# One array for rows and expert outputs, weights beside the last scatters, and the last batch in two halves

## What is computed

```python
x = x + tanh(g_xattn[0]) * attention(layernorm(x), ctx, ctx, bias=(b1 + b2 - b3) * side)   # 64 keys per batch
h = layernorm(x)
p = sigmoid(h @ Wr.T + rb)                       # 8 experts, the 2 best of each row, weighted by p
x = x + tanh(g_ffn[0]) * (expert(h, shared) + sum(p[e] * expert(h, e) for e in top2(p)))
        # expert(h, e) = (silu(h @ Wg.T) * (h @ Wu.T)) @ Wd.T, inner width 512
f = layernorm(x)
t = tanh(ctx @ Ws  [per text]  +  f @ W  [per row]  +  b)      # every row with each of 64 texts, 256 wide
att = softmax(t @ w + mask)
ws, bs = tanh(att @ ctx @ Wcw.T + bcw), tanh(att @ ctx @ Wcb.T + bcb)
x = x + tanh(g_xattn[1]) * (ws * f + bs)
q = clip(round(layernorm(x) / s), -127, 127)
x = x + tanh(g_ffn[1]) * (s * q @ (ternary - 1).T + bias)
```

## Time and profile before

| | |
|---|---|
| median of 3 runs | 1060.84 us (1059.93 to 1063.52) |
| profiled execution | 1066.61 us |
| its span | 1065.0 us |
| mean granted TensorE clock | 0.95 of full speed |
| busy share: TensorE, VectorE, ScalarE, GpSimd | 89%, 71%, 62%, 22% |
| one row tile's activation on ScalarE (L724) | 0.60 us |
| bytes moved by DMA | 220.81 MB |

### The profile page before, as it was taken

One profiled execution on the slowest core, in us unless ns is written; L12 is line 12 of the kernel. 1 busy time (PEld: TensorE's weight loads), 2 busy tenths in 40 slices (PEclk: granted clock), 3 DMA queues, 4 the chain that ended last, 5 costly groups with the idle time before them and its releaser, 6 DMA issues.

```text
span 1065.0 us, 22912 instructions
## 1 busy us (share of the span) xinstructions
PE 952.0 (89%) x8350; PEld 750.5 (70%) x8350; DVE 752.8 (71%) x2048; ACT 656.9 (62%) x893; POOL 229.8 (22%) x260
## 2 busy tenths in 40 slices
PE   5689998886999889999999999999999999986762
PEld 2447777675999877877777878878887887843331
DVE  2697777673222368879879969867875776697995
ACT  1122112110110029979999999969987986899991
POOL 1014344444012212122212312111211111120000
PEclk9689899998999999999999999999999999998886
DMA  8012999923999866656666666677776766410000
GB/s 262 25 55 97 396 407 390 340 70 135 333 349 327 295 224 232 231 171 223 207 220 218 216 219 229 235 244 239 272 259 217 256 229 228 150 32 21 2 21 21
DMA packets 138754, 220.81 MB, mean 207 GB/s; under 512 B 14129, under 2 KB 80178, under 8 KB 138642
## 3 DMA queue, kind: packets, MB, share of 16 engines
q1 hardware_dynamic: 120242, 157.59, 44.2%
q10 hardware_dynamic: 8464, 34.60, 8.3%
q0 software_dynamic: 9936, 27.15, 7.2%
HBM read 159.14 MB, written 60.16 MB: 206 GB/s over the span
## 4 chain that ended last, share of the span: by engine, by line
PE 50%; issue 6%; DVE 5%; DMA 1%; POOL 0%; POOLq 0%; DVEq 0%
PE bank L1289 20%; PE bank L1484 15%; PE bank L1458 10%; PE bank L1466 2%; PE bank L1411 1%; DVE tanhs L1132 1%; PE bank L1510 1%; PE bank L1336 1%; DVE arena L1132 0%; DMA picked<-expert_rows,slot_of 0%; DVE tanhs L1131 0%; DVE arena L1131 0%; DVE shared_w L1131 0%; DVE shared_w L1132 0%; DVE normed L912 0%
## 5 line engine op out<-in xcount | busy, mean ns | idle before, releaser
L1289 PE MATMUL bank<-rowsT,expert_w 128*128 128x128 f32 x2656 | 327.3, 277 | 1.9 <-issue 1.9
L1289 PEld LDWEIGHTS bank<-rowsT,expert_w 128*128 128x128 f32 x2656 | 318.0, 193 | 10.9 <-issue 7.4
L744 ACT ACTIVATE tanhs<-shared_w,txtT 128x512 f32<-128x512 f32 x268 | 169.7, 726 | 30.3 <-issue 19.8
L1458 PE MATMUL bank<-expert_w,act 128*128 128x256 f32 x664 | 160.7, 385 | 0.0
L645 POOL DMA_DIRECT2D expert_rows<-rows_out x71 | 44.7, 629 | 449.6 <-DVE rows_out L1089 425.5
L1458 PEld LDWEIGHTS bank<-expert_w,act 128*128 128x128 f32 x664 | 120.1, 190 | 30.3 <-issue 17.3
L744 ACT ACTIVATE arena<-shared_w,txtT 128x512 f32<-128x512 f32 x216 | 136.4, 728 | 0.0
L724 ACT ACTIVATE act<-bank 128x512 f32<-128x512 f32 x83 | 49.7, 599 | 131.5 <-PE bank L1289 126.6
L656 POOL DMA_INDIRECT picked<-expert_rows,slot_of x64 | 73.4, 1146 | 94.3 <-issue 55.4
L1089 DVE COPY rows_out<-bank 128x256 f32<-128x256 f32 x71 | 30.0, 422 | 89.5 <-PE bank L1458 89.4
L1484 PE MATMUL bank<-arena,pick_w 128*32 128x256 f32 x1320 | 85.8, 387 | 5.9 <-ACT arena L733 4.8
(11 more groups left out here) (267 smaller groups left out, 1414.3 us busy)
## 6 DMA issues: line engine op xcount, KB each, us to landing
expert_w<-in_WgT SPq DMA_DIRECT2D x71, 512.0 KB
expert_w<-in_WuT SPq DMA_DIRECT2D x71, 512.0 KB
expert_w<-in_WdT SPq DMA_DIRECT2D x71, 512.0 KB
expert_rows<-tanhs ACTq DMA_DIRECT2D x1, 33792.0 KB
rows_in<-rows_by_expert SPq DMA_DIRECT2D x71, 128.0 KB, 5.8
expert_rows<-rows_out POOLq DMA_DIRECT2D x71, 128.0 KB, 5.4
expert_w<-in_WgsT SPq DMA_DIRECT2D x12, 512.0 KB
expert_w<-in_WusT SPq DMA_DIRECT2D x12, 512.0 KB
```

Source lines behind the costliest of these rows:

```text
L744: got = e.activation(tiles[ec][:, S * j:S * (j + 1)], featT[ec], ACT.Tanh, bias=txtT[:, ec, t + j:t + j + 1])
L1289: got = e.matmul(bank[:, i * P:(i + 1) * P], w[:, at:at + P], t[:, c * P:(c + 1) * P], start=c == 0, stop=c == DC - 1)
L1458: got = e.matmul(row_bank[:, 0:D], act[n % 2][:, c * P:(c + 1) * P], w[:, at:at + D], start=c == 0, stop=c == IC - 1)
```

## The change

- The array `outs_dram` is gone. Expert outputs are stored to `rows_dram`, over the rows of their own tile, and gathered from there.
- `rows_dram` is set to zero before the scatters. `blank` now issues nine transfers on ScalarE's queue: for each batch b the part of all eight regions into which that batch's rows can be the first to come (4 MB), and the part for absent tiles (1 MB). They are placed at the start, ahead of the first attention steps. The scatters of batch b wait for part b, and the first fetch for the part of the absent tiles. `zero_rows`, `pads` and `pad` are gone, with their constants.
- The first `fetch` waits for the tile list and the constants, issues the weights of tiles 0 and 1, and only then waits for all scatters and loads rows.
- The last batch's second part is done in two groups of 256 rows. `groups` has nine entries in place of eight batches; the last two have 16 tanh tiles each, of 4 texts by 256 rows. `mix_in`, `feature`, `rho` and `mix_out` of such a group work on half the rows. The first half can begin when the first two of the batch's four row blocks are gathered, and its `mix_out` runs beside the second half's tanh tiles.
- `PAIRS`, `JOINS`, `PLACES` and `LAGS` have other values.

The diff, cut to its core:

```diff
-PAIRS = {0: 21, 1: 11, 2: 12, 3: 8, 4: 4, 5: 8, 6: 17, 7: 28}
-JOINS = {0: 8, 1: 8, 2: 8, 3: 16, 4: 19, 5: 12, 6: 1, 7: 0}
+PAIRS = {0: 17, 1: 12, 2: 10, 3: 0, 4: 0, 5: 0, 6: 18, 7: 24, 8: 10}
+JOINS = {0: 16, 1: 8, 2: 8, 3: 28, 4: 28, 5: 28, 6: 1, 7: 0, 8: 0}
...
+        self.groups = [(b, 0, ST) for b in range(B - 1)] + [(B - 1, 0, ST // 2), (B - 1, ST // 2, ST // 2)]
+        self.tiles = [T * n // 8 for _, _, n in self.groups]
...
+        tiles = self.tiles[g]
+        share = min(int(PAIRS[g]), tiles)
+        return m * share // tiles != (m + 1) * share // tiles
...
-        place([[("blank",)]], PLACES["blank"], PLACES["blank"])
+        place([[("blank",)]], -PLACES["att_norm"] - 19, -PLACES["att_norm"] - 19)
...
                     if r == 0:
                         e.wait_ge(s_tiles, 1)
-                        e.wait_ge(s_zeroed, 16)
-                        e.wait_ge(s_padded, 16 * E)
-                        for j in range(2):
-                            e.wait_ge(s_scattered[j], 32 * ST * B // 2)
+                        e.wait_ge(s_absent, 16)
...
-                    if r >= WEIGHTS:
+                        for q in range(2):
+                            fetch_weights(n_of[q])
+                        for j in range(2):
+                            e.wait_ge(s_scattered[j], 32 * ST * B // 2)
+                    elif r >= WEIGHTS:
...
                 elif name == "scatter":
                     b, i = k
                     e.wait_ge(s_placed, b + 1)
+                    if i == 0:
+                        e.wait_ge(s_zeroed[b], 16)
...
-                elif name == "pad":
-                    h, = k
-                    e.wait_ge(s_pads, 1)
-                    e.wait_ge(s_zero, 1)
-                    for j in range(h * E // 2, (h + 1) * E // 2):
-                        e.indirect_dma_start(
-                            out=rows_dram, out_offset=bass.IndirectOffsetOnAxis(ap=pad_at[:, j:j + 1], axis=0),
-                            in_=zero_tile[:, :], in_offset=None).then_inc(s_padded, 16)
...
-                    e.dma_start(outs_dram[bass.ds(tile * P, P), :], rows_out[r % OUTS][:, :]).then_inc(s_stored[r % OUTS], 16)
+                    e.dma_start(rows_dram[bass.ds(tile * P, P), :], rows_out[r % OUTS][:, :]).then_inc(s_stored[r % OUTS], 16)
...
                 elif name == "blank":
                     e.wait_ge(s_zeros, 1)
-                    e.dma_start(outs_dram.rearrange("(p n k) d -> p n (k d)", p=P, n=BLANKS),
-                                zeros.unsqueeze(1).to_broadcast([P, BLANKS, 1024])).then_inc(s_blank, 16)
+
+                    by_batch = rows_dram[0:ABSENT * P, :].rearrange("(e b p k) d -> b p e (k d)", e=E, b=B, p=P)
+                    for b in range(B):
+                        e.dma_start(by_batch[b], zeros.unsqueeze(1).to_broadcast([P, E, 1024])).then_inc(s_zeroed[b], 16)
+                    e.dma_start(rows_dram[ABSENT * P:, :].rearrange("(p n k) d -> p n (k d)", p=P, n=2),
+                                zeros.unsqueeze(1).to_broadcast([P, 2, 1024])).then_inc(s_absent, 16)
...
+                        cols_of, W = rows_of(g), P * groups[g][2]
+                        t = groups[g][0] * T + 2 * S // W * m
                         for ec in range(DC):
-                            for j in range(2):
-                                got = e.activation(tiles[ec][:, S * j:S * (j + 1)], featT[ec], ACT.Tanh, bias=txtT[:, ec, t + j:t + j + 1])
+                            for j in range(2 * S // W):
+                                got = e.activation(tiles[ec][:, W * j:W * (j + 1)], featT[ec][:, cols_of], ACT.Tanh,
+                                                   bias=txtT[:, ec, t + j:t + j + 1])
...
+                    for j in range(2 * S // W):
+                        got = e.tensor_scalar(w[:, W * j:W * (j + 1)], featT[ec][:, cols_of], txtT[:, ec, t + j:t + j + 1], None, ALU.add)
+                    got.then_inc(s_wide_in, 1)
```

More of the change, by code:

```diff
@@ L124, in route @@
             steps[-self.ST] += [("opened", 1)]
-            steps += [[("pads",)], [("tiles",)]] + [[("pad", h)] for h in range(2)]
+            steps += [[("tiles",)]]
         return steps
@@ L168, in added, with mix_out @@
[L168 to L176 removed]
+    def mix_out(self, g):
+        halves = range(self.groups[g][2] // 2)
+        return [[("rho", g)], [], [("turn_rho", g)], [("soft_rho", g)], [("rsum", g)], [("weigh_c", g)], [("squash", g)], [("stretch", g)],
+                [("power", "lin", g)], [("affine", g)], [("newton", "lin", g)], [("step", g)], *([("quantize", g, h)] for h in halves),
+                [("apply", g)], [("turn_q", g)], [("add_bias", g)], *([("linear", g, h)] for h in halves)]
```

503 lines of the change are left out of this document (269 added, 234 removed).

## The result

The changed kernel takes 1129.04 us (median; 1126.99 to 1131.62) against 1062.18 (1059.93 to 1066.47) for the kernel before on the same chip: a ratio of 1.0626, 95% interval 1.0583 to 1.0669. It is 66.9 us slower; the forecast was 18.7 us faster, and the range ended at 1061.

What follows compares the result with a forecast made beforehand. Bounds: TensorE and ScalarE in the batch stages, plus the 245 to 267 us seam. Terms -9.5 + 2 - 11.4 + 0.2 = -18.7 gave 1047.9 profiled, 1042 as median; range 1027 to 1061.

Steps and rivals of the forecast that it cites:

- 5.7 us in front of that copy: Start, ScalarE: nine zeroing issues at 0.63 us delay batch 0's first attention copy; taken as +4 us, bounds 0 and +6.
- a rival with 0.12: Start: ScalarE's queue holds it between zeroing issues, some 25 to 75 us later, 1068 to 1118, middle 1085; chance 0.12.
- Zeroing: First part: early zeroing issues cost +4 us, scatters no longer sharing the DMA engines give 2 back; together +2.
- taken as unchanged within 3 us: Row tiles before 392 us: assumed to keep their time within 3 us; slowing through the new order would prove it wrong.
- Seam, -9.5: Scatters to first row tile: pads gone and weights early, TensorE starts at 256.5 to 259 against 267.32; bounds 6 and 12.
- Joins and adds, -11.4: Tanh stages, mainly batches 3 to 5: more joins, fewer pre-added tiles give -14.4 us, less 3 for waits on VectorE.
- Last batch, +0.2: Last batch by halves: +5.2 ScalarE, -0.6 batch 6, +2 VectorE, -6.4 from a shorter end chain.
- a lead of eight buffers (18 us): Last batch: VectorE's 89 us of work fits ScalarE's 65 us plus this lead, about level, so +2, bounds 0 and +12.
- VectorE bounds the halves: Last batch: 256-column adds take 0.37 us, +12 in place of +2: 1052, with friction up to 1064; chance 0.08.
- joins give nothing: Tanh stages: VectorE's in-order waits turn TensorE's saving into idle time; 1050 to 1060, middle 1054; chance 0.20.
- does not do what it says: Seam: weights still start late because SyncE waits elsewhere, leaving only the pads' share, within the bound of 6; no chance given.
- More is freed: Scatters' "remote" idle times between 105 and 212 us go and batch 0 follows TensorE: 6 and 3 more, 1027 to 1033; chance 0.10.

Runs made afterwards that it cites:

- before_early: Kernel before with its single zeroing transfer issued at about 30 us in place of 103 us: 1053.9 us against 1054.88.
- before_same: The kernel before, unchanged, run again for its trace in the session of three later kernels: span 1057.2 us.
- after_spaced: Kernel after with its nine zeroing transfers issued one by one, each a batch's work ahead of its scatters, not back to back: 1044.47 us against 1054.88.
- spaced_whole: after_spaced with the last batch mixed whole again, with the kernel before's share of adds: 1049.67 us where the kernel before took 1067.0.

## Why the prediction was wrong

*The step that failed.* "At 0.63 us each that is 5.7 us in front of that copy." It was 64.7. The price came from a row of one transfer with nothing behind it, and I had written down the condition under which it doesn't hold as a rival with 0.12: decided "from the second issue on". It decides from the third at 4 MB. My ground against it, SyncE's "up to twelve 0.5 MB transfers under way at 0.4 us an issue", fails in the bytes: by what its queue had moved, at most some 2.7 MB of them were open at any issue among the row tiles of the kernel before (at 271 us). The rows said nothing on larger amounts. The rival's time was low too: the 1129 lie above even its upper end, 1118. A full hold was put at 87 us and discounted, but the 64.7 us reached the first scatter whole (147.6 against 80.2 spaced). In the first 105 us no other engine found more than 24 us of work while ScalarE stood.

*Zeroing, apart from that.* Its traffic costs nothing early (before_early). The +5 us to the first scatter beside the hold are 2 of GpSimd's order (80.6 against 78.5 in one session); the rest wasn't taken apart.

*The scatters.* +9.6 from first to last, and no term in the sum stood for it. The row tiles before 392 us, "taken as unchanged within 3 us", did hold (+0.6 from the first product to the first feature copy). I had named them as the place to look, not GpSimd's order in front of the scatters, though the planner's table has it moved (power for attention from -3.5 to -12.5). That order, with 2 to 8 us in the whole time, is the part of it that has a cause. The stretch gave back about what the seam had won: first scatter to first feature copy is 312.7 us before and 312.3 after.

*Seam, -9.5.* From last scatter's issue to the first row tile's product 22.0 us before and 11.3 after (324.76 to 336.09), -10.7. Its parts were wrong: I let the early weights do part of it, and they do next to nothing. The last scatter's landing was read off the pads as 3.5 us and took 5.9 beside the weights; the rows' landing, read as 5.3 us, is 2.0 in before_same (246.39 to 248.40), where the first product waits for the weights. The Trainium skill (DMA: Bandwidth & Descriptors, Queues, rings and completion order) says that descriptors on one engine are consumed in ring order; with it the prediction put the rows at the late end, 12 us after the first weights' issue. The trace agrees: on SyncE's queue 2.1 of the 3.1 MB of weights had moved when the rows were issued at 330.89, 3.1 MB by 333.7, and the rows landed at 335.09, 12.2 us after the weights' first issue at 322.86. But most of the delay came from the late issue of the rows, which the prediction had at 4.2 us behind the weights' and which came 8.0 behind.

*Joins and adds, -11.4.* Batches 3 to 5 gave -1.5, -4.4 and -7.0, so -12.9, against -14.4 without friction and -11.4 with. Batch 3's limit went from TensorE to ScalarE, 87.07 busy of 87.63, forecast 85.4; batches 4 and 5 are full on TensorE at 90.34, forecast 91 and 90. Batch 0 gained 3.4, which I had put at 0, just past my bound of 3. Over batches 0 to 5 this part gave -16.7 us.

*Last batch, +0.2.* It was +10.6, and whole it is 12.5 us faster. VectorE's load was right, 88.1 us from 1026.6 to the end against my 89, and so was the add: 6.38/24 = 0.27 us against 0.29 taken. The estimate from the figures of the Trainium skill (VectorE: DVE Perf Modes, Side-by-side) was 0.29 too, and the trace is 0.02 under it. A plain half tile took 3.2 us against 3.0. What failed is "a lead of eight buffers (18 us)": the wait at the feature copy takes it away. Even with the lead, 89 us of work in 65 + 18 leave 6 us over, which the sum took as +2. And one sum over both halves hides that the first, with all 16 tiles pre-added, loads VectorE for 45.6 us against ScalarE's 35.5. The rival "VectorE bounds the halves" so had the right engine, but not through a dearer add. The end chain did what was said, 16.3 us from the last tanh, forecast 16, before 22.4.

*The rival "joins give nothing"* is out, as is *"does not do what it says"*. *"More is freed"*: idle stretches that end with "remote" were not the zeroing's; they are still there after (51.5 us in each trace), and whether they appear goes with the session (below).

With the hold and the order mended and the last batch left as it was, the change gives -24 to -32 us, against the -18.7 forecast. The 0.50 on the forecast rested on an issue price that no row of two transfers in a row had shown.

## What to carry to other kernels

Before several large transfers are issued in a row by an engine that also computes, count the bytes already handed to its queue: behind some 5 MB the engine itself stood here, and whatever waited for it, and 1 MB transfers back to back cost 1.3 us and more each, from the third on, even below that. Issue them one at a time, each when the one before has moved, or as one transfer. When an edit comes with a new order of instructions, price every step that passes a wait on an in-order engine, and test a lead that is read off a number of buffers against the wait that opens it.

## What the runs showed of the hardware

A transfer of 34.6 MB takes the issuing engine 0.63 us; two of half its size 34.4, nine parts 64.7 to 67.6, 33 parts 73.5. A queue's issue time so says nothing about the next one's.

The kernel before, unchanged, took 167.5 us from first to last scatter in one trace and 154.2 in another. The first has 51.5 us of idle time ended by "remote" between 60 and 340 us (ScalarE's and VectorE's added), the second none. The kernel after has 51.5 too, after_spaced none, and spaced_whole, with the same first part, 56.2: it took 180.6 us in place of 160.1. Such a stretch in spaced_whole:

```profile
88.64 0.37 ACT L749 ACTIVATE odds<-bank,router_b 128x128 f32<-128x128 f32 x1 [9.73 <-remote]
```

Meanwhile GpSimd issues batch 0's eight scatters (80.07 to 90.13). The kernels of one session all had these stretches or all had none, so they don't belong to a kernel. Nor do they belong to a chip: of two sessions on the same chip the four kernels of the first had none (after_spaced among them) and the four of the second all had them (spaced_whole among them). What they are was not found. Each of these first-part differences can so be trusted only inside a session.
